# Storing the next batch's q and k at the seam between two FFNs, and a small SiLU at the head of the projection's stage

## The reference

```python
def attention(teacher_logits, teacher_features, Wq, bq, Wk, bk):
    query = jnp.einsum('bnc,dc->bnd', teacher_features, Wq) + bq
    key = jnp.einsum('bnc,dc->bnd', teacher_features, Wk) + bk
    attention = jax.nn.softmax(jnp.einsum('bnd,bmd->bnm', query, key), axis=-1)
    return jnp.einsum('bln,bmn->blm', teacher_logits, attention)

def ffn(hidden_states, gate_cp, up_cp, down_cp):
    gate_w, up_w, down_w = (spline_reconstruct(c) for c in (gate_cp, up_cp, down_cp))
    gate = jnp.einsum('bsh,ih->bsi', hidden_states, gate_w)   # 512 -> 2048
    up = jnp.einsum('bsh,ih->bsi', hidden_states, up_w)
    inter = jax.nn.silu(gate) * up
    return jnp.einsum('bsi,hi->bsh', inter, down_w)           # 2048 -> 512

x = x + attention(layernorm(x), ctx, Wq, bq, Wk, bk)
x = x + ffn(layernorm(x), gate_cp, up_cp, down_cp)
```

## Time and profile before

| | |
|---|---|
| median of three runs | 271.87 us (271.04 to 272.04) |
| the profiled execution | 271.57 us |
| its span, first to last instruction | 269.8 us |
| PE busy | 251.6 us, 93% |
| DVE, ACT, POOL busy | 184.4, 127.1, 132.4 us |
| mean granted clock of TensorE | 0.967 |

### The profile page before, as it was taken

The page is one execution under the profiler, slowest core; times in us unless marked ns, Lnnn a source line. Parts: engine busy times, 40 slices in busy tenths (PEclk is TensorE's granted clock), DMA queues, the critical chain, the costliest instruction groups (busy, mean ns, idle before and its releaser), DMA issues.

```text
span 269.8 us, 4108 instructions
## 1 busy us (share of the span) xinstructions
PE 251.6 (93%) x1386; PEld 169.6 (63%) x1388; DVE 184.4 (68%) x326; ACT 127.1 (47%) x205; POOL 132.4 (49%) x138
## 2 busy tenths in 40 slices
PE   7889649999899999999999999999999999599995
PEld 2223136855464868885747688847476889286784
DVE  0698996698567876864678768646787686465533
ACT  3035542325479651336796513367966132354320
POOL 0498626187792831314938413149374131487800
PEclk9977977999999999999999999999999999989999
DMA  6999008000090000022720000227000002200004
GB/s 197 315 428 416 30 16 298 1 0 2 10 372 9 0 4 2 0 78 78 292 97 0 0 0 0 78 78 287 24 0 0 0 0 78 78 2 0 0 2 156
DMA packets 7354, 23.11 MB, mean 86 GB/s; under 512 B 1200, under 2 KB 2480, under 8 KB 5936
## 3 DMA queue, kind: packets, MB, share of 16 engines
q1 hardware_dynamic: 7344, 22.98, 23.0%
HBM read 18.78 MB, written 4.19 MB: 85 GB/s over the span
## 4 chain that ended last, share of the span: by engine, by line
PE 78%; DVE 10%; ACT 4%; DMA 2%; issue 2%; POOL 1%; SPq 1%; DVEq 0%; ACTq 0%; POOLq 0%
PE bank L1318 12%; PE bank L1321 11%; PE bank L1363 11%; PE bank L1335 6%; PE bank L1170 6%; PE bank L1267 5%; PE bank L1269 5%; PE bank L1268 5%; PE bank L1181 4%; DVE prod L867 4%; PE bank L1370 3%; PE bank L1224 3%; DMA power<-in_g_power 2%; PE bank L1282 1%; PE bank L1347 1%
## 5 line engine op out<-in xcount | busy, mean ns | idle before, releaser
L1120 POOL TENSOR_TENSOR ih<-inter,ones 128x512 fp32r<-128x512 f32 x64 | 65.2, 1042 | 24.7 <-DVE inter L958 24.5
L958 DVE TENSOR_TENSOR inter<-inter,bank 128x512 f32<-128x512 f32 x64 | 43.4, 686 | 25.2 <-ACT inter L772 20.2
L772 ACT ACTIVATE inter<-bank 128x512 f32<-128x512 f32 x64 | 37.7, 600 | 23.8 <-PE bank L1321 23.7
L1363 PEld LDWEIGHTS bank<-d_r,ih 128*128 128x128 f32 x256 | 31.0, 191 | 7.7 <-issue 6.7
L1363 PE MATMUL bank<-d_r,ih 128*128 128x192 f32 x256 | 32.2, 275 | 0.0
L1318 PE MATMUL bank<-xh,gate_r 128*128 128x512 f32 x64 | 29.1, 455 | 1.5 <-DVE zg L950 1.5
L743 ACT ACTIVATE qk<-bank,nmr,rstd 128x512 f32<-128x512 f32 x16 | 12.5, 780 | 37.0 <-PE bank L1269 20.0
L1104 POOL TENSOR_TENSOR xres<-x,ones 128x2048 f32<-128x2048 f32 x4 | 14.4, 3602 | 23.9 <-DMA out<-xres 23.6
L1318 PE MATMUL bank<-xh,up_r 128*128 128x512 f32 x64 | 26.1, 408 | 0.0
L1321 PE MATMUL bank<-zg,up_v 102*128 102x512 f32 x64 | 26.1, 408 | 0.0
L1321 PE MATMUL bank<-zg,gate_v 102*128 102x512 f32 x64 | 25.8, 404 | 0.0
(11 more groups left out here) (103 smaller groups left out, 450.1 us busy)
## 6 DMA issues: line engine op xcount, KB each, us to landing
x<-in_x SPq DMA_DIRECT2D x4, 1024.0 KB, 4.9
xT<-in_xT SPq DMA_DIRECT2D x4, 1024.0 KB, 6.9
out<-xres SPq DMA_DIRECT2D x16, 256.0 KB, 2.1
ctxT<-in_ctxT SPq DMA_DIRECT2D x4, 512.0 KB, 7.4
rd<-in_d_r SPq DMA_DIRECT2D x2, 768.0 KB, 6.4
knots<-in_d_knot SPq DMA_DIRECT2D x1, 1280.0 KB, 11.6
d_coef<-in_d_coef SPq DMA_DIRECT2D x1, 1024.0 KB, 14.3
d_pt<-in_d_node SPq DMA_DIRECT2D x1, 1024.0 KB, 15.7
```

The lines of the kernel that those rows point to most:

```text
L772: nc.scalar.activation(inter[:, m], gbank[m % 2][:], ACT.Silu).then_inc(s["silu_done"], 1)
L958: V.tensor_tensor(inter[:, m], inter[:, m], ubank[m % 2][:], ALU.mult).then_inc(s["mult_done"], 1)
L1120: G.tensor_tensor(ih[:, m], inter[:, m], ones[:, 0].broadcast_to([P, TOK]), ALU.mult).then_inc(s["ih_done"], 1)
L1363: mm(in_blocks(obank[t][:], i // CLS), ih[:, m, t * P:(t + 1) * P], d_r[:, i], start=m == 0, stop=False, skip_group_check=True)
```

## The change

A tile `spare` (128x4) is added. At the head of `project` ACT runs a SiLU of the constant tile eps into it. The stage `between`, in which ACT and DVE did the replication's Copy and remainder, goes; the call of `st.qk(a)` takes its place, and the call behind the four `activate` goes. In ACT's `qk` the replication's Copy now stands between the Identity for q and the Identity for k; in DVE's and POOL's `qk` the old `between` is done (nothing, on POOL). PE's `qk` always had the replication between q and k. DVE, PE, POOL and SP issue the same instructions in the same order as before.

```diff
--- before.py
+++ after.py
+        spare = sb("spare", [P, NT], f32)
...
             st.project(b)
             if a is not None:
-                st.between(a)
+                st.qk(a)
             else:
                 st.replicate(b)
             for m in range(4):
                 st.activate(b, m)
-            if a is not None:
-                st.qk(a)
             for m in range(4):
                 st.gate_up(b, m)
...
                 def qk(b):
                     for n in range(2):
+                        if n == 1 and not first(b):
+                            Stages.replicate(b - 1)
                         act.wait_ge(s["qk_mm"], 2 * b + n + 1)
                         if n == 0:
                             act.wait_ge(s["bqk_in"], 2 * 16)
-                            if not (isinstance(b, int) and b == 0):
+                            if not first(b):
                                 act.wait_ge(s["x1_added"], NT * b)
                         nc.scalar.activation(qk_[:, n], abank[n][:], ACT.Identity, bias=bqk[:, n:n + 1]).then_inc(s["qk_done"], 1)
...
                 def project(b):
+                    if first(b):
+                        act.wait_ge(s["consts_set"], 1)
+                    nc.scalar.activation(spare[:], eps[:], ACT.Silu)
                     act.wait_ge(s["zp_mm"], b + 1)
                     nc.scalar.activation(zp[:, 0], zgbank[:], ACT.Copy).then_inc(s["zp_hi"], 1)
-
-                def between(b):
-                    Stages.replicate(b - 1)
...
                 def qk(b):
-                    pass
+                    if not first(b):
+                        Stages.replicate(b - 1)
```

## The result

The changed kernel takes 267.93 us (median of four runs, 267.60 to 268.40), the kernel before on the same chip 271.61: a ratio of 0.9879, 95% interval 0.9854 to 0.9903. A second comparison gave 267.66 against 271.07, again 0.9879 (0.9841 to 0.9916).

A forecast was written before the change was run, and what follows sets the result against it. PE, holding 78% of the chain, was taken as the bound. 1.64 us from the stumble less 2 x 0.10 us in the heads gave 1.44 us, from the median 271.87 to 270.43 us; range 269.7 to 271.4.

The forecast's parts named there:

- The stumble at tile 6: In gate_up of the three loop passes PE waits for late SiLUs; moving the Identities gains all 1.64 us.
- The second table load: At the seam's head the load ahead of the first SiLU disappears; that SiLU waited for PE anyway: worth zero.
- The spare SiLU: In the head, ahead of the Copy to zp; delays it by 0.10 us at the second and third seam.
- q's Identity: In the head, ahead of the Copy to zg; delays it 0.10 us, on the spare SiLU's chain, so not added.
- The first seam: Ahead of the first loop pass: the Copy to zp waited 0.38 us for PE, so the spare costs nothing.
- the last FFN's head: Seam without q and k: the spare runs under PE's projection and costs nothing.
- k's Identity: In the head, ahead of SiLU 0: makes it 0.07 us late, hidden since PE needs product 0 only later.
- The gain turns into another wait: Rival, chance 0.07: PE waits longer for the exponentials at tile 9; all 1.64 us is lost, 272.1 us.
- the head eats half: Rival, chance 0.17: Identities and spare run without overlap, or the spare costs more; gain falls to 0.4 to 1.0 us.
- The kinder clock at the end: Rival, chance 0.06: the slow stretch ahead of the last FFN moves or vanishes, up to another 1.64 us, 268.8.
- the rival of the slower clock: Chance 0.07 with others of that sign: PE idling slows its clock at the other three seams, 275.4 us.
- the signs of being wrong that were named: Late replication, zg's Copy held, wait for product 0, longer exponentials wait, tile 6 stumble, clock falling at first three seams.

The follow-up runs named there:

- spare only: The kernel before with the spare SiLU alone, the Identities left behind the fourth SiLU: 270.65 us, ratio 0.9994.
- move only: The changed kernel without the spare SiLU, so only the two Identities are moved: 271.85 us, ratio 1.0031 to the kernel before.
- n = 5: The changed kernel with five more matmuls a pass, ahead of the attention's product of its first tile: 271.12 us, ratio 1.0010 to the kernel before.
- zg first: The changed kernel with the Copy to zg ahead of both Identities: 267.87 us, ratio 0.9888 to the kernel before.
- both filled kernels: Kernel before and changed kernel, each with q and k computed once more in PE's two gaps ahead of the last FFN: 269.18 and 268.04 us.

## Why the prediction was wrong

- *The stumble at tile 6.* Right, and a little more: 1.86 us in three passes where 1.64 was taken. It had been counted at the pace of 0.2336 us a matmul; without the stumble the pace is 0.2306 (7.15 over 31), another 0.09 us in the second and third pass. What makes it faster stays open.
- *The second table load, worth nothing.* Right for the order of before (spare only), wrong as a statement on the new order: there the load would stand behind k's Identity and cost 1.17 us a pass (move only). The sum was not touched, since both edits come together.
- *The spare SiLU, 0.10 us, and q's Identity, in one chain and not added.* The rule holds, a size doesn't. The spare alone costs the head 0.06 us (5.31), q's Identity alone 0.19 (move only, 5.44), both together 0.20 (5.45): the larger hides the smaller. The Identity was taken at 0.10 because it was to start when the trace has q's matmuls end, 3.01 us behind the projection; it starts at 3.10 (120.03 to 123.13), with the spare or without it. So the heads cost 0.40 us in all and not 0.20. (The 0.24 for an Identity without overlap is 0.02 more than its rows give, 124.38 and 0.69 less 124.85; it changes nothing.)
- *The first seam, the last FFN's head and k's Identity cost nothing.* Right: 6.53 in both, 5.14 and 5.09, and no wait for product 0.
- *The gain turns into another wait; the head eats half.* Neither. The wait for the exponentials is still 0.4 us.
- *The sum.* 1.44 us forecast, 1.46 by the traces of what the change touches, and a pass of 53.68 us (125.48 to 179.16) where about 53.7 was named. The mechanism was right; that the size fits to 0.02 is luck, since 0.22 more from the stumble and 0.20 more in the heads cancel. And it is not the whole time.
- *The kinder clock at the end.* This is the step that failed. It stood among the rivals with its place and its price (up to 1.64 us; 1.63 came in the tail), but with a chance of 0.06, as something that "nothing in the profile says". The sum put it at nothing: the slow stretch of the last FFN was left in the time as if it belonged to the seam, and no reason was given why it should outlast a shift of 1.4 us. The runs show that the gaps are only half of its cause: a shift of the seam by some 1.5 us to earlier removed it (186.12 and 186.36 to 184.86 and 184.59), one by 0.7 us back restored it. The same error stands in the rival of the slower clock, which has it decided by PE idling "for over a microsecond": gaps of 1.53 and 1.47 us left the clock alone in the changed kernel and with n = 5. Of the ten traces with both gaps six fall and four don't, so that in hindsight the rival deserved about an even chance. None of the signs of being wrong that were named looks at the last seam, and none of them came.
- *The range* left that rival outside (268.8), and the time came at 267.9.

## What to carry to other kernels

Where PE idles just ahead of a stretch at the lower clock, that stretch is a term of its own. Here it came or went with edits that moved the seam by 0.7 to 3.5 us, and it hid or doubled what the edit itself is worth. Fill such gaps (useless matmuls in the two gaps were worth 1.8 us here) before two kernels are compared, or compare stretch by stretch in the traces. And an edit that is worth nothing alone, as the early table load, can be what another needs: here each of the two alone gave nothing or a loss.

## What the runs showed of the hardware

Eight of the ten experiments' profiles have both gaps of about 1.5 us ahead of the last FFN. Behind them the granted clock fell to 0.50 in five, and stayed at 1.00 in the three others (the changed kernel, n = 5, zg first); it stayed at 1.00 in both filled kernels. Delays of 0.7 and 1.4 us brought the fall back, 3.5 us took it away, and the time from the clock's last rise to the seam sorts the traces that fall from those that don't. On ACT a 128x4 ACTIVATE lasts 0.20 to 0.21 us, and the next operation starts 0.11 us after its start; a table load lasts 1.28 us and the next operation starts 0.01 to 0.02 us behind it.
